# A graph network layer pair on one core: the last stage's linear product moved into the second edge layer

## The chip, the cores and the metric

The kernel runs on 1 core of one Trainium2 chip. The metric is the device time of one execution in microseconds, median of several.

## The reference, cut to what matters

12,500 nodes of 256 numbers, 200,000 edges sorted by destination, 8 heads of 32. A first attention layer over the edges with a feed-forward part gives x. Then:

```
h    = relu(layernorm(x))                      # x: 12500 x 256
h_in = h @ W_lin + b_lin                       # the linear product
feat = (h_in @ W_gat) as 8 heads of 32;  el, er = sums of feat * attn_l, feat * attn_r
e    = leaky_relu(el[src] + er[dst], 0.2)      # 200000 x 8
a    = softmax of e over the edges of one dst
out  = segment_sum(feat[src] * a, dst) + gat_bias
x    = x + h_in + leaky_relu(out, 0.01)
```

All arithmetic is fp32.

## The kernel before

**Stages.** A query, key and value stage over 98 node tiles of 128 nodes (to about 700 us), the first edge layer (to 2750), the node stage with the feed-forward part and the tables of the second layer (to about 3700), the second edge layer (to 5760), the output stage (to 5932).

**Edge layer.** The edges are cut into 782 spans of 256. Work goes in steps, one span against one node tile; a span that straddles two tiles is taken twice, which gives 880 steps in 110 blocks of 8 (`NB`, `ST`). POOL gathers two times 128 rows of `ft_tab` for each span (`gathers`, L531), 1564 gathers a layer, into a ring of 32 spans in `Gf` (`SLOTS`); a slot comes free when the weighed rows of its step are made (`ev_made`). SP loads for each step the row of destinations (`dst_rows`, L452), and passes on to DVE that the rows of a step have landed (`landed`, `rows_rdy`), ten steps behind its loads (`RLAG`). All engines walk the same loop of blocks B and steps s, written out by hand, in order:

- DVE: `el_er` at s (L1218), `members` of step s+6 (L1230), `weigh` of step s-12 (L1287), `add` of step s-14 (L1302), and once a block `leaky` and `scores` at 7, `chunk_scans` of the block before at 0 (L1242), `row_scans` at 1 (L1254), `whole_scans` at 2, `below_maximum` at 3, `rescaled` at 6.
- PE (helpers at L822 and L825): `scores_turned` of the block before at 0, `spread` of step s+2, `agg` of step s-12, then `row_values` at 0, `columns` at 1, `maxima_turned` at 2, `rescale` at 3, `links_turned` at 5.
- ACT (copies at L588): `distances` (L627) and `onehots` (L633) of later steps, `er_rows` of step s+4, `row_values` at 1 (tile `wlf`), `links` at 6 (tile `ats`), and the stores of the sums (L701).

DVE's `chunk_scans` wait for the transposed scores of the block (`s_tr`). PE's `row_values` wait for both scans (`scan_a`), use bank 7, and ACT's `row_values` copy them out for DVE's `row_scans`. Bank 7 also takes `links_turned` (columns 0 to 127), which ACT reads into `ats`.

**Node stage.** It stores for each tile the normalised input transposed (`h2t_tab`) and x with b_lin added (`xm_tab`).

**Output stage.** For each tile ACT loads a tile of `xm_tab` and of `h2t_tab` (L809, L810), six tiles ahead (`FR`); SP loads the sums (L479). PE forms the linear product out of two halves and adds `xm` with the identity as third product, into bank t % 3. DVE divides the sums by their denominator (L1460, L1469, L1478), POOL adds the bias (L582), DVE makes the leaky relu (L1473) and adds PE's bank (L1466) into one of three output buffers; ACT stores it (L816).

Of the kernel before, what the change touches and what calls it, by code (L numbers as in the profile page):

```python
# [22 lines left out]
ALU = mybir.AluOpType  # L23
# [30 lines left out]
RLAG = (6, 10)  # L54
FR = 6
assert all(m * DIV >> 16 == m // SLOTS[0] for m in range(NS))
assert NB % 2 == 0 and NB >= 6 and NS > NSPAN + NT - 1
# [80 lines left out]
def build(nc, x, last, edges, span_src, Wq, Wk, Wv, Wp, bp, g1, b1n, g2, b2n, W1, b1, W2, b2,  # L138
          Wl, bl, Wg, al, ar, gb, out):
    ctx = ExitStack()  # L140
    with ctx:
# [14 lines left out]
        xm_tab = dram("xm_tab", (NPAD, D))  # L156
        h2t_tab = dram("h2t_tab", (NPAD, D))
        sums = dram("sums", (NS * P, HV))
        dst_tab = dram("dst_tab", ((LC * P + 1) * SPAN,))
# [100 lines left out]


        used[0] = 0
        w_l = steps[:, 0:2 * D].rearrange("p (k n) -> p k n", k=2)
        v_gb = steps[:, 2 * D:3 * D]
        fin_h = [carve(D) for _ in range(FR)]
        fin_in, fin_xm = [[carve(w) for _ in range(FR)] for w in (HV, D)]
        fin_a, fin_b, fin_p, fin_o, fin_d = [[carve(w) for _ in range(3)] for w in (D, D, D, D, 2 * H)]
# [15 lines left out]
        for name in """const_made gather_free stats_made setup_loaded path_dve path_pe w_loaded  # L283
            q_x0 q_x1 q_x2 q_x3 q_dve q_rstd q_relu q_tr q_hT q_mm q_ka q_st0 q_st1 q_st2 q_st3 q_vq
            rec_ld rec_f slots sel_made x_mm x_cp fields mask_made er_made tables span_rdy rows_rdy
            m_w m_wge m_acc m_h m_x m_dve0 m_dve1 m_dve2 m_var1 m_var2 m_var3 m_rs1 m_rs2 m_rs3
            m_tr0 m_tr1 m_tr2 m_cp0 m_cp1 m_cp2 m_mm0 m_mm1 m_mm2 m_w1 m_gelu f_tr f_cp f_mm f_w
            m_sxm m_sh2 m_sft m_rdacc m_fo m_xmb f_lin m_xb m_hb m_h1b f_in0 f_in1 f_in2 f_in3 f_in4 f_in5 f_max f_rec f_att f_bias f_lr f_out f_st0 f_st1 f_st2""".split():
            S_[name] = sem(name)
# [44 lines left out]
        def _(sp):  # L334
# [119 lines left out]
            def span_rows(b):  # L454
# [3 lines left out]
                    skip_runtime_bounds_check_because="a step's span is one of the spans or the one after them")[1]  # L458

            sp.wait_ge(S_["rec_ld"], 16 * (LC + 1))  # L460
            for u in range(NS + RLAG[1]):
                if u < NS:
                    if u % ST == 0:
                        at = span_rows(u // ST)
                    dst_rows(Blk(u // ST, 1), u % ST, at[u % ST])
# [5 lines left out]
            for par in range(2):  # L471
                sp.wait_ge(acs[1][par], 32 * (NB // 2))


# [111 lines left out]
        def _(act):  # L586
# [110 lines left out]
            def sum_store(layer, B, h):  # L697
# [4 lines left out]
                              acc[:, B.par, 4 * h:4 * h + 4, :]).then_inc(acs[layer][B.par], 16)  # L702

            def er_rows(B, s):

# [4 lines left out]
            def edge_phase(layer):  # L710
                def turn(B):
                    A = B.on(-1)
                    for s in range(ST):
# [33 lines left out]
                        if s == 3 and A.live:  # L747
                            weights(A)

                z = Blk(0, layer)  # L750
# [53 lines left out]

            for t in range(NT + FR):
                if t < NT:
                    k = t % FR
                    wait(act, S_["f_lin"], t - FR + 1)
                    act.dma_start(fin_xm[k], xm_tab[t * P:(t + 1) * P, :]).then_inc(S_[f"f_in{k}"], 16)  # L809
                    act.dma_start(fin_h[k], h2t_tab[t * P:(t + 1) * P, :]).then_inc(S_[f"f_in{k}"], 16)  # L810
                u = t - FR
                if u < 0:
# [7 lines left out]
        def _(pe):  # L820
# [90 lines left out]
            def scores_turned(B):  # L911
                pe.wait_ge(E_["smade"], B.c + 1)
                tr(bank[6][:, 1:P + 1], S[:, :]).then_inc(E_["s_tr"], 1)

            def row_values(B):

                pe.wait_ge(E_["scan_a"], 2 * B.c + 2)
                for q, v in enumerate((wa[:, 0:1], scan1[:, P - 1:P], scan2[:, 0:1])):
# [21 lines left out]
            def edge_phase(layer):  # L940
                def turn(B):
                    A = B.on(-1)
                    for s in range(ST):
# [20 lines left out]
                        if s == 5 and B.live:  # L964
                            links_turned(B)

                z = Blk(0, layer)
# [73 lines left out]
            edge_phase(1)  # L1041

            for t in range(NT):
                k = t % FR
                o = bank[t % 3][:, 0:D]
                pe.wait_ge(S_[f"f_in{k}"], 48 * (t // FR + 1))
                wait(pe, S_["f_out"], t - 2)
                for c in range(2):
                    mm(o, fin_h[k][:, c * P:(c + 1) * P], w_l[:, c, :], c == 0, False)
                mm(o, ident[:, :], fin_xm[k], False, True).then_inc(S_["f_lin"], 1)  # L1050

        @block.vector
        def _(dve):
# [400 lines left out]
            def f_turn(t):  # L1456
                if t < NT:
                    k, d, src = t % FR, fin_d[t % 3], hv(fin_in[t % FR])
                    dve.wait_ge(S_[f"f_in{k}"], 48 * (t // FR + 1))
                    V.tensor_scalar(d[:, 0:H], src[:, :, HD], 1e-30, None, ALU.max).then_inc(S_["f_max"], 1)  # L1460
                if t >= 3:
                    u = t - 3
                    dve.wait_ge(S_["f_lin"], u + 1)
                    dve.wait_ge(S_["f_lr"], u + 1)
                    wait(dve, S_[f"f_st{u % 3}"], 16 * (u // 3))
                    V.tensor_tensor(fin_o[u % 3], fin_p[u % 3], bank[u % 3][:, 0:D], ALU.add).then_inc(S_["f_out"], 1)  # L1466
                if t < NT:
# [51 lines left out]
```

## Time and profile before

| | |
|---|---|
| median of 3 runs | 7285.09 us (7285.01 to 7289.17) |
| span of the profiled execution, first to last instruction | 5932.0 us |
| time of the profiled execution around its span | not shown; median less span is 1353.1 us |
| PE busy | 5400.5 us, 91% |
| DVE busy | 4947.5 us, 83% |
| POOL busy | 3753.2 us, 63% |
| ACT busy | 3081.2 us, 52% |
| mean granted TensorE clock | 0.896 |
| moved by DMA | 1313.63 MB, 221 GB/s |

How to read it: the profile is of one execution and covers 5932.0 us of it. Engines are PE (TensorE; PEld its weight loads), DVE (VectorE), ACT (ScalarE), POOL (GpSimd) and SP (SyncE, which here issues DMAs only). A name with q, as ACTq, is the engine's queue: it issues a DMA or waits. The ends of matmul records are modelled, so their durations overlap the next ones; their starts are as recorded. An fp32 product shows as two records. Granted clock 1.00 is 2.4 GHz, 0.50 is 1.2 GHz. Idle time has the name of what ended it; "issue" is time in which the engine waited for nothing that the profile shows.

### The profile page before, as it was taken

The numbers are of one execution on the slowest core, as the hardware profiler recorded it, in microseconds if no ns is written. First come the engines' busy times: TensorE is split into PE (matmuls) and PEld (weight loads), VectorE is DVE, ScalarE is ACT, GpSimd is POOL, SyncE is SP. The second block draws the span as 40 slices with busy tenths as digits, with TensorE's granted clock in tenths as the row PEclk, the third lists the DMA queues.
The fourth block names the chain that finished last, engine by engine and source line by source line (L and its number), as shares of the span: only waits on it lengthen the run. The fifth ranks groups of instructions, "written<-read, shape, count | busy, mean of one in ns | idle before, by whom it ended". The sixth has DMA issues, their size and how long they took to land. (4 is left out here: it accounts for less than half of the span.)

```text
span 5932.0 us, 127571 instructions
## 1 busy us (share of the span) xinstructions
PE 5400.5 (91%) x25898; PEld 4282.1 (72%) x25898; DVE 4947.5 (83%) x12562; ACT 3081.2 (52%) x10078; POOL 3753.2 (63%) x4022
## 2 busy tenths in 40 slices
PE   8978888888888888887999998999999999999988
PEld 5556666666666666666999997777777777777766
DVE  4469999999999999996777775788787788887878
ACT  3445666666666666652333334555565565555540
POOL 1147667767766766653444445777777777777754
PEclk9999999999999999998999998777777777777779
DMA  5669898989998988873222223777777787777869
GB/s 176 212 222 293 280 288 286 292 283 287 286 286 285 288 284 283 281 255 100 83 85 85 83 85 109 213 224 221 220 218 218 218 221 219 222 219 220 220 198 311
DMA packets 723029, 1313.63 MB, mean 221 GB/s; under 512 B 109087, under 2 KB 502131, under 8 KB 722420
## 3 DMA queue, kind: packets, MB, share of 16 engines
q0 software_dynamic: 200192, 634.41, 37.8%
q1 hardware_dynamic: 416578, 396.48, 22.3%
q10 hardware_dynamic: 105650, 276.43, 12.3%
q14 instruction: 448, 3.67, 0.2%
q8 instruction: 161, 2.64, 0.2%
HBM read 964.16 MB, written 342.73 MB: 220 GB/s over the span
## 5 line engine op out<-in xcount | busy, mean ns | idle before, releaser
L822 PE MATMUL bank<-ev,oh 128*128 128x264 f32 x7040 | 2303.2, 457 | 88.8 <-DVE ev L1287 88.3
L531 POOL DMA_INDIRECT Gf<-kv_tab,srcs x1564 | 1582.7, 1012 | 710.4 <-issue 496.7
L531 POOL DMA_INDIRECT Gf<-ft_tab,srcs x1564 | 1592.6, 1018 | 484.1 <-issue 411.3
L822 PEld LDWEIGHTS bank<-ev,oh 128*128 128x128 f32 x7040 | 1474.2, 222 | 347.0 <-DVE ev L1287 124.0
L1287 DVE TENSOR_TENSOR ev<-Gf,ex 128x528 f32<-128x528 f32 x1760 | 1228.5, 698 | 1.6 <-ACT ex L695 1.2
L822 PE MATMUL bank<-Gf 128*128 128x128 f32 (+3 forms) x6284 | 1193.7, 343 | 4.5 <-ACT Gf L588 3.3
L822 PE MATMUL bank<-qs,oht 128*128 128x256 f32 x3520 | 955.7, 394 | 226.7 <-DVE prod L1196 226.4
L627 ACT ACTIVATE absd<-lane,dlocs 128x128 f32<-128x128 f32 x3520 | 1112.7, 389 | 3.8 <-DVE bms L1169 3.8
L822 PEld LDWEIGHTS bank<-Gf 128*128 128x128 f32 x6284 | 935.4, 191 | 170.4 <-issue 98.4
L822 PEld LDWEIGHTS bank<-qs,oht 128*128 128x128 f32 x3520 | 599.6, 190 | 437.1 <-issue 371.4
L1302 DVE SCALAR_TENSOR_TENSOR acc<-acc,same,bank 128x264 f32<-128x264 f32 x1540 | 732.3, 475 | 31.5 <-PE bank L822 28.6
L508 POOL TENSOR_TENSOR vr<-vr,mhalf 128x1 f32<-128x1 f32 x392 | 248.6, 634 | 717.1 <-DVE vr L1378 418.6
L633 ACT ACTIVATE oh<-absd,ones 128x512 f32<-128x512 f32 x880 | 631.6, 718 | 10.9
L1196 DVE TENSOR_TENSOR prod<-Gf,bank 128x512 f32<-128x512 f32 x880 | 594.9, 676 | 18.6 <-SPq L395 18.3
L1202 DVE TENSOR_REDUCE sred<-prod 128x16 f32<-128x512 f32 x880 | 590.5, 671 | 0.3
L588 ACT ACTIVATE oht<-bank 128x512 f32<-128x512 f32 x440 | 261.1, 594 | 299.3 <-PE bank L825 296.1
L822 PEld LDWEIGHTS bank<-erq,prod 128*128 128x128 f32 x1760 | 362.5, 277 | 68.4 <-issue 33.2
L777 ACT ACTIVATE Gf<-bank,Gf 128x128 f32<-128x128 f32 x784 | 223.5, 368 | 290.9 <-PE bank L822 290.9
L822 PE MATMUL bank<-erq,prod 128*128 128x8 f32 x1760 | 351.9, 310 | 19.8 <-DVE sred L1218 19.2
L659 ACT ACTIVATE rm<-bank,oh 128x8 f32<-128x8 f32 x220 | 78.6, 357 | 530.2 <-PE bank L822 524.2
L822 PEld LDWEIGHTS bank<-erq,oht 128*128 128x128 f32 x1760 | 270.0, 213 | 58.3 <-issue 25.9
L670 ACT ACTIVATE ats<-bank 128x128 f32<-128x128 f32 x220 | 61.0, 277 | 468.6 <-PE bank L825 468.6
(158 smaller groups left out, 6134.7 us busy)
## 6 DMA issues: line engine op xcount, KB each, us to landing
sums<-acc ACTq DMA_DIRECT2D x440, 528.0 KB
qs<-q_tab SPq DMA_DIRECT2D x880, 128.0 KB
qs<-dst_tab SPq DMA_DIRECT2D x880, 128.0 KB
Gf<-sums SPq DMA_DIRECT2D x196, 132.0 KB, 2.6
kv_tab<-Gf SPq DMA_DIRECT2D x98, 260.0 KB, 2.1
Gf<-in_x SPq DMA_DIRECT2D x196, 128.0 KB, 2.2
Gf<-kv_tab,srcs POOLq DMA_INDIRECT x1564
Gf<-ft_tab,srcs POOLq DMA_INDIRECT x1564
```

The lines of the kernel that those rows point to most:

```text
L508: pool.tensor_tensor(vr[:, 2 * k + 1:2 * k + 2], vr[:, 2 * k:2 * k + 1], mhalf[:, :], ALU.pow).then_inc(done, 1)
L531: pool.indirect_dma_start(out=rows[layer][:, m % SLOTS[layer], k, :], out_offset=None, in_=tab, in_offset=bass.IndirectOffsetOnAxis(ap=src ...
L588: act.activation(o, i_, ACT.Copy).then_inc(s, 1)
L627: act.activation(absd[:, g % 2, k, :], lane[:, :], ACT.Abs, scale=-1.0, bias=dloc[:, B.n, 4 * g + k:4 * g + k + 1]).then_inc(E_["ohd"], 1)
L633: act.activation(oh[:, (B.c * 4 + g) % OHG, :, :].rearrange("p c n -> p (c n)"), absd[:, g % 2, :, :].rearrange("p c n -> p (c n)"), ACT.R ...
L659: act.activation(rm[:, B.par, :], bank[7][:, 392:392 + H], ACT.Identity, scale=oh0[:, B.par, 0:1], bias=oh0[:, B.par, 1:2]).then_inc(E_["r ...
L777: act.activation(gT[:, f * P:(f + 1) * P], bank[2 + f // 4][:, (f % 4) * P:(f % 4 + 1) * P], ACT.Gelu, bias=v_b1[:, f:f + 1]).then_inc(S_[ ...
L822: return nc.tensor.matmul(o, a, r, start=first, stop=end)
L1196: V.tensor_tensor(prod[:, s % 2, :, :], step_rows(0, at)[:, :, 0:D], bank[2 + s % 2][:, :].rearrange("p (k n) -> p k n", k=2), ALU.mult).t ...
L1202: V.tensor_reduce(hc(sred[:, :])[:, :, 2 * s:2 * s + 2].rearrange("p h c -> p c h"), prod[:, s % 2, :, :].rearrange("p k (h w) -> p k h w" ...
L1287: V.tensor_tensor(weighed(B, s).rearrange("p k (h w) -> p k h w", h=H), val.rearrange("p k (h w) -> p k h w", h=H), hc(ex[:, B.par, :])[:, ...
L1302: V.scalar_tensor_tensor(acc[:, B.par, s, :], prev, same[:, B.n * ST + s:B.n * ST + s + 1], sums_bank(B, s), ALU.mult, ALU.add).then_inc(E ...
```

## The change

The three products of a tile are formed in the second edge layer, one tile a block: PE at the end of step 7 into bank 7, ACT copies them to SBUF at the end of its step 7, SP stores them to a new table `r_tab` and loads the inputs two tiles ahead. The output stage loads `r_tab`, eight tiles ahead, in place of `xm_tab` and `h2t_tab`, and DVE adds it from SBUF.

```diff
+RR = ST
+        r_tab = dram("r_tab", (NPAD, D))
+        used[0] = SLOTS[1] * 2 * WIDTH[1]
+        res_h, res_xm, res_o = [[carve(D) for _ in range(2)] for _ in range(3)]
...
-        fin_h = [carve(D) for _ in range(FR)]
-        fin_in, fin_xm = [[carve(w) for _ in range(FR)] for w in (HV, D)]
+        fin_in, fin_r = [[carve(w) for _ in range(n)] for n, w in ((FR, HV), (RR, D))]
...
@@ block.sync
+            def res_turn(b):
+                if b >= 0:
+                    sp.wait_ge(S_["res_cp"], b + 1)
+                    sp.dma_start(r_tab[b * P:(b + 1) * P, :], res_o[b % 2]).then_inc(S_[f"res_st{b % 2}"], 16)
+                t = b + 2
+                if 0 <= t < NT:
+                    for v, tab in ((res_h, h2t_tab), (res_xm, xm_tab)):
+                        sp.dma_start(v[t % 2], tab[t * P:(t + 1) * P, :]).then_inc(S_[f"res_in{t % 2}"], 16)
             for u in range(NS + RLAG[1]):
+                if u % ST == 0 and u // ST - 3 < NT:
+                    res_turn(u // ST - 3)
...
@@ block.scalar
+            def residual(t):
+                act.wait_ge(S_["res_mm"], t + 1)
+                wait(act, S_[f"res_st{t % 2}"], 16 * (t // 2))
+                copy(res_o[t % 2], bank[7][:, 0:D], S_["res_cp"])
...
+                        if s == 7 and layer == 1 and B.n < NT:
+                            residual(B.n)
...
-            for t in range(NT + FR):
+            for par in range(2):
+                act.wait_ge(S_[f"res_st{par}"], 16 * (NT // 2))
+            for t in range(NT + RR):
                 if t < NT:
-                    k = t % FR
-                    wait(act, S_["f_lin"], t - FR + 1)
-                    act.dma_start(fin_xm[k], xm_tab[t * P:(t + 1) * P, :]).then_inc(S_[f"f_in{k}"], 16)
-                    act.dma_start(fin_h[k], h2t_tab[t * P:(t + 1) * P, :]).then_inc(S_[f"f_in{k}"], 16)
+                    k = t % RR
+                    wait(act, S_["f_out"], t - RR + 1)
+                    act.dma_start(fin_r[k], r_tab[t * P:(t + 1) * P, :]).then_inc(qld[k], 16)
...
@@ block.tensor
+            def residual(t):
+                pe.wait_ge(S_[f"res_in{t % 2}"], 32 * (t // 2 + 1))
+                pe.wait_ge(E_["ats_made"], NB + t + 1)
+                o = bank[7][:, 0:D]
+                for c in range(2):
+                    mm(o, res_h[t % 2][:, c * P:(c + 1) * P], w_l[:, c, :], c == 0, False)
+                mm(o, ident[:, :], res_xm[t % 2], False, True).then_inc(S_["res_mm"], 1)
             def row_values(B):
+                if B.layer == 1:
+                    pe.wait_ge(S_["res_cp"], min(B.n + 1, NT))
...
+                        if s == 7 and layer == 1 and B.n < NT:
+                            residual(B.n)
...
@@ block.tensor, the output stage
-            for t in range(NT):
-                k = t % FR
-                o = bank[t % 3][:, 0:D]
-                pe.wait_ge(S_[f"f_in{k}"], 48 * (t // FR + 1))
-                wait(pe, S_["f_out"], t - 2)
-                for c in range(2):
-                    mm(o, fin_h[k][:, c * P:(c + 1) * P], w_l[:, c, :], c == 0, False)
-                mm(o, ident[:, :], fin_xm[k], False, True).then_inc(S_["f_lin"], 1)
@@ block.vector
-                    dve.wait_ge(S_[f"f_in{k}"], 48 * (t // FR + 1))
+                    dve.wait_ge(S_[f"f_in{k}"], 16 * (t // FR + 1))
-                    dve.wait_ge(S_["f_lin"], u + 1)
+                    dve.wait_ge(qld[u % RR], 32 * NB + 16 * (u // RR + 1))
-                    V.tensor_tensor(fin_o[u % 3], fin_p[u % 3], bank[u % 3][:, 0:D], ALU.add)
+                    V.tensor_tensor(fin_o[u % 3], fin_p[u % 3], fin_r[u % RR], ALU.add)
```

## Rows read from the trace of the kernel before

**Rows 1.** The page: its span, and the granted clock in 40 equal slices.
```profile
span 5932.0 us, 127571 instructions
PEclk9999999999999999998999998777777777777779
```

**Rows 2.** Windows: busy us of PE, PEld, DVE, ACT, POOL; clock, DMA share, GB/s.
```profile
3700.00:4900.00 1200.00, 1121.98 (x4681) 889.79 (x4680) 958.18 (x2719) 705.22 (x2595) 924.14 (x906) 0.73 0.78 219
4900.00:5725.00 825.00, 776.75 (x3243) 616.42 (x3242) 665.25 (x1886) 487.32 (x1793) 634.94 (x624) 0.72 0.79 219
...
5800.00:5900.00 100.00, 92.20 (x384) 68.03 (x384) 84.35 (x319) 0.00 (x0) 46.44 (x64) 1.00 1.03 336
```

**Rows 3.** Waits, 4900 to 5725 us: who for whom, us in total, times, longest.
```profile
POOL Gf L531 <- issue: 162.2, 532, 0.3
...
DVE scan L1242 <- PE bank L825: 59.8, 44, 1.9
DVE sred L1218 <- PE bank L822: 45.5, 100, 0.8
...
PE bank L822 <- DVE ev L1287: 33.0, 132, 0.6
...
DVE sred L1218 <- SPq L395: 4.0, 10, 0.7
```

**Rows 4.** Tile S, 3700 to 5760 us: count, ns min/median/max, first and last start.
```profile
L825 PE MATMUL bank<-ident,S x109: 272/273/421, 3703.4 to 5744.0; 128*128 128x128 f32 x109
```

**Rows 5.** Windows over one and a half blocks, cut where the granted clock changes.
```profile
4792.80:4803.00 10.20, 9.85 (x31) 7.72 (x30) 8.70 (x24) 3.98 (x14) 8.07 (x8) 0.50 0.77 198
4803.00:4813.20 10.20, 9.09 (x54) 7.20 (x52) 8.57 (x27) 8.59 (x32) 7.76 (x9) 1.00 0.87 261
4813.30:4823.50 10.20, 10.18 (x30) 8.14 (x31) 7.95 (x23) 4.36 (x18) 7.76 (x9) 0.50 0.69 194
```

**Rows 6.** Timeline of PE around a block's end: start us, us, what, records.
```profile
4804.98 1.14 PE L822 MATMUL bank<-ev,oh 128*128 128x264 f32 x4
4805.95 0.27 PE L825 MATMUL bank<-ident,S 128*128 128x128 f32 x1
...
4807.40 0.27 PE L825 MATMUL bank<-ident,wa 128*1 128x128 f32 x1
```

**Rows 7.** Timeline of DVE and ACT there; in brackets the idle time before.
```profile
4806.26 0.42 DVE L1242 TENSOR_TENSOR_SCAN scan<-ats,bank 128x128 f32<-128x128 f32 x1 [1.18 <-PE bank L825]
4806.36 1.26 ACT L627 ACTIVATE absd<-lane,dlocs 128x128 f32<-128x128 f32 x4
...
4807.93 0.48 ACT L588 ACTIVATE wlf<-bank 1x384 f32<-1x384 f32 x1 [0.20 <-PE bank L825]
```

**Rows 8.** Timeline of PE in the output stage, one tile and the next.
```profile
5911.38 1.09 PE L822 MATMUL bank<-steps,Gf 128*128 128x256 f32 x4
5912.31 0.59 PE L822 MATMUL bank<-Gf,ident 128*128 128x256 f32 x2
5912.74 1.10 PE L822 MATMUL bank<-steps,Gf 128*128 128x256 f32 x4
```

**Rows 9.** Groups of PE, 3700 to 5740 us: busy us, mean ns, idle before.
```profile
L822 PE MATMUL bank<-ev,oh 128*128 128x264 f32 x3455 | 1356.5, 530 | 82.0 <-DVE ev L1287 81.8
```

**Rows 10.** Groups, 0 to 700 us: ACT's copies of 128x256 out of PSUM.
```profile
L588 ACT ACTIVATE Gf<-bank 128x256 f32<-128x256 f32 x196 | 68.4, 373 | 22.9 <-PE bank L822 22.8
```

**Rows 11.** Tile out: issues of its stores, ns min/median/max, first and last start.
```profile
L816 ACTq DMA_DIRECT2D out<-Gf x98: 338/443/1090, 5773.3 to 5925.1; - x98
```

**Rows 12.** Waits of SP's queue, 3760 to 5740 us.
```profile
SPq L395 <- POOLq L538: 881.1, 494, 5.6
```

**Rows 13.** Timeline of DVE in the output stage: the first instruction of two turns.
```profile
5911.95 0.16 DVE L1460 TENSOR_SCALAR Gf<-Gf 128x8 f32<-128x8 f32 x1
...
5913.38 0.16 DVE L1460 TENSOR_SCALAR Gf<-Gf 128x8 f32<-128x8 f32 x1
```

More of the change, by code:

```diff
@@ L287, in build @@
             m_tr0 m_tr1 m_tr2 m_cp0 m_cp1 m_cp2 m_mm0 m_mm1 m_mm2 m_w1 m_gelu f_tr f_cp f_mm f_w
-            m_sxm m_sh2 m_sft m_rdacc m_fo m_xmb f_lin m_xb m_hb m_h1b f_in0 f_in1 f_in2 f_in3 f_in4 f_in5 f_max f_rec f_att f_bias f_lr f_out f_st0 f_st1 f_st2""".split():
+            m_sxm m_sh2 m_sft m_rdacc m_fo m_xmb m_xb m_hb m_h1b f_in0 f_in1 f_in2 f_in3 f_in4 f_in5 res_in0 res_in1 res_mm res_cp res_st0 res_st1 f_max f_rec f_att f_bias f_lr f_out f_st0 f_st1 f_st2""".split():
             S_[name] = sem(name)
@@ L472, in _ @@
                 sp.wait_ge(acs[1][par], 32 * (NB // 2))
+                sp.wait_ge(S_[f"res_st{par}"], 16 * (NT // 2))
             def f_load(t):
@@ L803, in _ @@
             edge_phase(1)
-            for t in range(NT + FR):
+            for par in range(2):
+                act.wait_ge(S_[f"res_st{par}"], 16 * (NT // 2))
+            for t in range(NT + RR):
                 if t < NT:
-                    k = t % FR
-                    wait(act, S_["f_lin"], t - FR + 1)
-                    act.dma_start(fin_xm[k], xm_tab[t * P:(t + 1) * P, :]).then_inc(S_[f"f_in{k}"], 16)
-                    act.dma_start(fin_h[k], h2t_tab[t * P:(t + 1) * P, :]).then_inc(S_[f"f_in{k}"], 16)
-                u = t - FR
+                    k = t % RR
+                    wait(act, S_["f_out"], t - RR + 1)
+                    act.dma_start(fin_r[k], r_tab[t * P:(t + 1) * P, :]).then_inc(qld[k], 16)
+                u = t - RR
                 if u < 0:
@@ L1462, in f_turn @@
                     u = t - 3
-                    dve.wait_ge(S_["f_lin"], u + 1)
+                    dve.wait_ge(qld[u % RR], 32 * NB + 16 * (u // RR + 1))
                     dve.wait_ge(S_["f_lr"], u + 1)
                     wait(dve, S_[f"f_st{u % 3}"], 16 * (u // 3))
-                    V.tensor_tensor(fin_o[u % 3], fin_p[u % 3], bank[u % 3][:, 0:D], ALU.add).then_inc(S_["f_out"], 1)
+                    V.tensor_tensor(fin_o[u % 3], fin_p[u % 3], fin_r[u % RR], ALU.add).then_inc(S_["f_out"], 1)
                 if t < NT:
```

## Prediction, made before the changed kernel ran

> **What bounds the kernel now.** I read the page first, for the span and the slices of the clock, then the busy times by stretch, then in the stretch that gets new work the waits, the order of one block and the clock, and last the stretch that loses work. The span is 5932.0 us [rows 1] and the median of the runs is 7285.09 us. The profile shows nothing of the 1353.1 us between the two; I take them as unchanged, so all sums are made on the 5932.0 us and added to 7285.09. About 0.2%, 15 us, is what a measurement of this kernel can tell from no change.
>
> The second edge layer runs from about 3700 to 5760 us and the output stage from there to the end. In the layer [rows 2] PE is busy 94% of the time (776.75 of 825 us), DVE 81%, POOL 77%, ACT 59%, the DMA engines 79%. Two paces lie very close together. POOL starts 624 gathers in 825 us, one each 1.322 us; its idle time is almost all "issue", 532 times 0.3 us, a fixed pause [rows 3]. So POOL runs without a stop: 1564 gathers in 110 blocks are 14.2 a block, 18.8 us. The consumers have their own pace: the scores of a block are transposed 109 times between 3703.4 and 5744.0 us, one each 18.9 us [rows 4]. Are they held back by the rows that POOL brings? From 4900 us on, no: DVE waits for rows 4.0 us in 825, but for PE 59.8 us in chunk_scans (L1242) and 45.5 us in el_er (L1218) [rows 3]. A later PE would not be hidden by a wait for data.
>
> PE in turn waits 33.0 us in these 825, for DVE's weighed rows [rows 3], and half of its time it is slow: 10.2 us at granted clock 0.50 (1.2 GHz), 10.2 us at 1.00 (2.4 GHz), 10.2 at 0.50 again, once each block [rows 5]. PE is busy 9.85 and 10.18 of 10.20 us at half clock, and starts 31 and 30 records there against 54 at full clock. The order in a block: DVE makes the scores, PE transposes them at the top of step 0, and DVE has stood idle for it 1.18 us when its scan starts at 4806.26 [rows 6, 7]. PE had no idle time there: it was in the aggregation of step 7, at 4804.98, until the transposition at 4805.95. So from about step 4 to step 0 of the next block PE sets the time, and around steps 1 to 3 DVE does.
>
> **The change, part by part.**
>
> *PE, in the layer.* Three products per tile are added at the end of step 7, in 98 of 110 blocks: exactly ahead of the transposition for which DVE waits. Price: at full clock the same six records start 1.36 us before the next tile's (5911.38 to 5912.74) [rows 8]. 98 x 1.36 = 133 us. Ends: at half clock twice that, 2.72 us a block, 267 us (the aggregation's mean of 530 ns over the layer [rows 9], against records 0.24 us apart at full clock in rows 6, shows what half clock does); and nothing, if the products slip into PE's waits. I take full clock, since in the traced block the clock had risen at 4803.0, three microseconds before the place where they go in [rows 5, 6], and I take the whole price, since PE has no wait just ahead of that place and DVE has one just behind it.
>
> *ACT, in the layer.* At the end of step 7 it waits for the products and then copies 128x256 out of PSUM. The copy of that shape took 373 ns [rows 10]: 98 x 0.37 = 37 us on an engine that is busy 59%. Behind this wait on ACT's queue are step 0's four distances (1.26 us) and one er copy, and then row_values, for whose copy DVE waits next. In the traced block row_values found ACT idle for 0.20 us [rows 7]. With the products PE's row transpositions come 1.36 us later, at 4808.8, and ACT, which goes on only at about 4807.4, needs 0.4 + 1.3 + 0.2 us and gets there at 4809.3, where it would have been on time with PE at 4809.3 (4807.93 plus 1.36). It is a tie; I cost it at nothing, with up to 0.3 us a block, 29 us, as its bound, and not below nothing.
>
> *PE's new waits.* The wait for ats_made is for a copy that ACT makes right after step 5's transposition. Behind it would queue all of PE, but ACT waits for that transposition and not the reverse. The wait in row_values for the copy out of bank 7 comes after one spread and one aggregation, 1.45 us by rows 6 (4805.95 to 4807.40), and the copy needs 0.5: covered. If ACT were late, PE would stand there and DVE's scan of the row behind it.
>
> *SP.* A block gets one wait, one store and two loads of 128 KB, some 0.45 us of SP each, as on ACT [rows 11]. Ahead of the change SP waits 881 us of the layer for landings [rows 12], so 1.4 us a block lie in that. The wait for res_cp of block b stands ahead of step 8b+24 on SP. To have passed the dst load of step 8b+23 SP needs the membership rows that DVE makes at step 8b+9, and DVE is there only after the scan of step 8b+8, which waits for a transposition that PE makes behind the products of block b: the copy is out or nearly so, and SP hardly waits. What is queued behind it are dst loads and the notice of landed rows, and DVE would wait for both. 384 KB in 19 us add 21 GB/s to 219 GB/s at a DMA share of 0.79 [rows 2]: 0.07 of share, hidden behind a lookahead of six steps and more.
>
> *POOL.* Nothing is added. With consumers 1.36 us a block slower, POOL's lead grows until the ring of 32 spans is full, and it then waits: that costs nothing, for the consumers set the end.
>
> *Output stage.* Removed per tile: three products, one load of 128 KB of two, a wait of DVE for PE. Stores go out from 5773.3 to 5925.1, 97 intervals of 1.565 us [rows 11]. In that time a tile moves 516 KB (132 of sums, three of 128), at 336 GB/s and a share of 1.03 [rows 2]: the transfers fill the engines. Afterwards it moves 388 KB, which at that rate is 1.18 us a tile. Late next is DVE: its five instructions follow each other without a gap, L1460 at 5911.95 and again at 5913.38, 1.43 us [rows 13]; ACT's queue, three issues of 0.44 us [rows 11], goes to two. So 1.43 for 1.565: 98 x 0.135 = 13 us saved. Ends: nothing, if the stores' landing still holds DVE through the three output buffers, and 24 us, if DVE's 84.35 us busy in 100 us [rows 2] (64 tiles, 1.32 each) could be closed up. The last add now reads SBUF in place of PSUM; I leave its time. The first load of sums waits for the layer's last stores as before.
>
> Sum: 133 - 13 = 120 us, so 7285 + 120 = 7405 us.
>
> **The clock, by a rule.** The trace has the clock rise once a block while PE is busy all the time at 1.2 GHz, and fall after the stretch where DVE sets the pace [rows 5]. So the clock answers to what PE does, and the new products are six dense records. The Trainium skill, "TensorE: Matmul & The Clock Gate", in its part on the clock gate, says that the slow clock is the resting state and that sustained matmul activity releases it. By that rule more work in a block could buy more time at 2.4 GHz. What speaks against much of it here: the products are put in where the clock is mostly up already, and the stretch behind which it falls, steps 1 to 3, keeps its gaps.
>
> **The rivals.**
>
> *A. The clock pays part of it.* Mean clock 0.72 [rows 2] is 56% of the time at half clock, 10.5 us of a block. If that fell to one half of the time, 9.4 us, PE would gain 0.55 us a block and 0.81 would be left: 98 x 0.81 - 13 = 66, 7351 us. For it: the rule above and the clock's answer to load. This is the rule's own outcome; I give it 0.14.
>
> *B. The products are hidden, and the kernel is faster.* Place: PE's waits for DVE between steps 1 and 3, with DVE's waits for rows in the first half of the layer. If PE catches up inside them, or the clock gives all of it back, the layer stays at POOL's 18.8 us a block and only the output stage counts: 7285 - 13 = 7272, at best 7261. It decides from the point where the 1.36 us are made good before the next block's transposition; PE's waits of 33.0 us in 44 blocks are 0.75 a block, too little alone. 0.10.
>
> *C. The products run at half clock.* If the clock's rise comes after step 7 in most blocks, each costs 2.72 us: 267 - 13 = 254, 7539 us. For it: 56% of the time is at half clock; against: [rows 5, 6]. 0.10.
>
> *D. It is not only PE.* ACT's wait or SP's three DMAs delay the chain by another 0.3 us a block: 120 + 29 = 149, 7434 us. 0.16.
>
> **How the numbers follow.** The forecast, full clock and whole price, has 0.50: 7405 us, its own range 7370 to 7440 (1.0 to 1.7 us a block, with both ends of the output stage's gain). Range 7320 to 7480: it holds the forecast, D, nearly all of A, and C where only part of the blocks are slow; left out are B and C proper. Faster by over 0.2% needs B with more than 15 us: 0.07. Within 0.2%: the rest of B and the low end of A: 0.07. Slower: 0.86.
>
> **What would show it.** Scores transposed each 20.2 us in place of 18.9; DVE's wait at L1242 up from 1.4 us a block (59.8 in 44) to about 2.7; the same clock pattern; POOL waiting for DVE's weighed rows from the middle of the layer; output stores 1.43 us apart at some 270 GB/s, and PE silent there. Wrong if transpositions stay 18.9 us apart (B), if the mean clock of the layer is well over 0.72 (A), if the new records take over 400 ns (C), or if ACT's wlf copy or DVE's el_er waits more while PE idles (D).

## The result and the profile after

The changed kernel took 7306.81 us (median of 5, 7302.19 to 7330.29), the kernel before, beside it, 7285.01 us (median of 5, 7270.14 to 7289.17): a ratio of 1.0044, 95% interval 1.0029 to 1.0059. That is 22 us slower by the medians, 21 to 43 by the interval. I had said 7405 us and at least 7320. The sign is right, the size by the medians is a fifth of the 120 us that I gave.

One thing must be known to read the numbers. The kernel before takes one of two times: about 7290 us in this result and in the first set of experiments, which ran on one chip, about 5940 us on the two other chips of the later sets. The trace that I had read (span 5932.0 us [rows 1]) is of the second kind, the times beside it are of the first. I call them the slow and the quick chip; that it is the chip, and not something else that differs between the sets, is not shown. Each ratio is against runs of the kernel before in the same set. Single executions fall out on a quick chip too: of the kernel before one of 16 took 6083.7 us at a mean granted clock of 0.794, of the step 2 kernel below one of 11 took 17555.13 us at 0.28, and the ratios leave both out. The first view is the changed kernel's page, its span and the granted clock in 40 slices:

```profile
span 7328.5 us, 128076 instructions
...
PEclk9978898889888998889999976666776666766675
```

That execution took 7330.29 us, so 1.8 us lie around its span, and not 1353.1. The missing 1353 us are inside the span. The page of the kernel before, run again unchanged on the slow chip (median 7295.63 us, this execution 7308.77), says the same:

```profile
span 7306.9 us, 127571 instructions
...
PEclk9978898889988988898999985666666666666679
```

Its second edge layer (slices 25 to 38) is at 0.5 to 0.6 where [rows 1] has 0.7 (slices 26 to 39). How far apart the blocks are, is in tile S: the line of DVE's mask of the scores, once a block (count, ns min/median/max, first and last start). After, on the slow chip:

```profile
L1241 DVE TENSOR_TENSOR S<-slk,bms x110: 277/284/340, 4402.9 to 7136.1; 128x128 f32<-128x128 f32 x110
```

Before, on the slow chip:

```profile
L1211 DVE TENSOR_TENSOR S<-slk,bms x110: 278/284/339, 4411.2 to 7117.6; 128x128 f32<-128x128 f32 x110
```

109 intervals of 25.1 us against 24.8, where [rows 4] had 18.9: the layer grew by 26.8 us (2733.2 less 2706.4), and blocks are 5.9 us longer on this chip already without the change. Each figure is of one traced execution; the same layer without products took 2698.6 us in the trace of the output stage alone, so the growth is known to some 8 us. Where much of that lies is seen at a block's end, in the timeline of the changed kernel (start us, us, engine, line; in brackets the idle time before and what ended it):

```profile
5514.39 1.14 PE L849 MATMUL bank<-ev,oh 128*128 128x264 f32 x4
...
5515.36 1.03 PE L849 MATMUL bank<-steps,Gf 128*128 128x256 f32 x4
...
5516.23 0.59 PE L849 MATMUL bank<-Gf,ident 128*128 128x256 f32 x2
...
5516.66 0.27 PE L852 MATMUL bank<-ident,S 128*128 128x128 f32 x1
...
5519.22 0.95 POOL L549 DMA_INDIRECT Gf<-ft_tab,srcs  x1 [0.30 <-issue]
5521.70 0.38 ACT L606 ACTIVATE Gf<-bank 128x256 f32<-128x256 f32 x1 [6.78 <-remote]
5521.74 0.42 DVE L1272 TENSOR_TENSOR_SCAN scan<-ats,bank 128x128 f32<-128x128 f32 x1 [7.40 <-remote]
```

The three products (lines 2 and 3) start 1.30 us before the transposition of the scores, near the 1.36 priced from [rows 8]. But then ACT and DVE do nothing for 4.8 us: the transposition is over at 5516.93, and both ACT, which waits for the products, and DVE, which waits for the transposition, start at 5521.7. PE's records go on to 5518.3 and POOL's gathers to 5520.2; after that all four engines stand. The wait's releaser is given as "remote", a name that no wait in the trace of [rows 3] has. It stands where the instruction that gives the signal had ended long before it. The semaphore events in the trace show the signals themselves: those of the products and of the transposition come at 5521.68 and 5521.72, though their records end at 5516.82 and 5516.93. Many blocks have such a pause, in the first edge layer too (its 109 intervals take 2902.2 us here, 431.2 to 3333.4, and 2274.7 on a quick chip). In the waits of 4500 to 7100 us (engine, name and line, releaser: us in total, times, longest) the changed kernel has

```profile
POOL Gf L549 <- DVE ev L1317: 654.3, 213, 7.6
...
DVE scan L1272 <- remote: 338.2, 51, 8.8
...
DVE scan L1272 <- PE bank L852: 112.4, 29, 5.8
```

and the kernel before, there,

```profile
POOL Gf L531 <- DVE ev L1287: 620.7, 203, 7.5
...
DVE scan L1242 <- remote: 387.1, 64, 8.7
...
DVE scan L1242 <- PE bank L825: 41.2, 22, 4.1
```

So before, POOL already waited for the consumers (in [rows 3] nearly all of its idle time was "issue"), and the "remote" pause at the scores was longer and more frequent before than after. Some of it only changed its name: with the rows named PE and the 27.0 and 53.5 us of "issue" at this scan, DVE waits there 455.3 us before and 504.1 after, 0.5 us a block more for products of 1.30. The change filled part of a hole that my trace didn't have.

The output stage didn't get shorter. Its stores, after:

```profile
L843 ACTq DMA_DIRECT2D out<-Gf x98: 338/454/1136, 7166.2 to 7321.3; - x98
```

97 intervals of 1.599 us, 1.571 before on this chip (7147.9 to 7300.3) and 1.565 in [rows 11]. I had said 1.43. A stretch of it (columns as in rows 2):

```profile
7180.00:7240.00 60.00, 0.00 (x0) 0.00 (x0) 59.98 (x186) 0.00 (x0) 33.88 (x38) 0.50 0.85 246
```

The transfers came down from a share of 1.03 to 0.85 and PE is silent, both as forecast; DVE fills the whole time.

### The profile page after: what moved, and what is told of

It reads as the page before. It is cut to its first block and busy times, and to the rows that moved or that the text cites. A ratio compares the mean times of both kernels' runs of the same rounds, so it can differ in the third digit from the quotient of the medians.

```text
span 7328.5 us, 128076 instructions
## 1 busy us (share of the span) xinstructions
PE 5826.4 (80%) x25898; PEld 4585.5 (63%) x25898; DVE 4999.3 (68%) x12562; ACT 3123.1 (43%) x10176; POOL 3704.4 (51%) x4022
## 3 DMA queue, kind: packets, MB, share of 16 engines
q1 hardware_dynamic: 458914, 435.04, 20.2%
## 5 line engine op out<-in xcount | busy, mean ns | idle before, releaser
L849 PE MATMUL bank<-ev,oh 128*128 128x264 f32 x7040 | 2500.1, 489 | 101.1 <-DVE ev L1317 71.3
L549 POOL DMA_INDIRECT Gf<-kv_tab,srcs x1564 | 1502.6, 961 | 1450.6 <-DVE ev L1317 938.6
L849 PEld LDWEIGHTS bank<-ev,oh 128*128 128x128 f32 x7040 | 1593.0, 240 | 400.3 <-DVE ev L1317 103.3
L849 PE MATMUL bank<-qs,oht 128*128 128x256 f32 x3520 | 1037.7, 421 | 225.6 <-issue 136.2
L849 PEld LDWEIGHTS bank<-qs,oht 128*128 128x128 f32 x3520 | 663.7, 210 | 426.9 <-issue 346.6
L852 PE MATMUL bank<-ident,oh 128*128 128x128 f32 x1760 | 317.6, 309 | 247.4 <-ACT oh L651 218.1
L1272 DVE TENSOR_TENSOR_SCAN scan<-ats,bank 128x128 f32<-128x128 f32 x220 | 91.6, 417 | 609.8 <-remote 429.7
L849 PEld LDWEIGHTS bank<-erq,prod 128*128 128x128 f32 x1760 | 391.6, 299 | 72.8 <-issue 46.9
L849 PEld LDWEIGHTS bank<-erq,oht 128*128 128x128 f32 x1760 | 319.9, 249 | 178.5 <-issue 141.0
L606 ACT ACTIVATE Gf<-bank 128x256 f32<-128x256 f32 (+1 forms) x494 | 185.0, 385 | 570.8 <-remote 290.0
```

What stands on the lines that cost most here:

```text
L549: pool.indirect_dma_start(out=rows[layer][:, m % SLOTS[layer], k, :], out_offset=None, in_=tab, in_offset=bass.IndirectOffsetOnAxis(ap=src ...
L606: act.activation(o, i_, ACT.Copy).then_inc(s, 1)
L849: return nc.tensor.matmul(o, a, r, start=first, stop=end)
L852: return nc.tensor.transpose(o, i_, ident[:, :])
L1272: V.tensor_tensor_scan(scan1[:, :], ats[:, 0:P], bank[6][:, 1:P + 1], -BIG, ALU.add, ALU.max).then_inc(E_["scan_a"], 1)
```

## The experiments

### On the slow chip: the kernel before, the output stage alone, the products twice

**The kernel before, unchanged**, for its profile beside the changed one's.

> The kernel before, unchanged, for a trace taken like that of the changed kernel, whose span of 7328.5 us covers its whole time while the first trace of before covered 5932.0 of 7285. Theory P (the products lie whole on the path of PE in the layer): the layer takes some 90 to 130 us less here than in the changed kernel, and the output stage that much more than in it. Theory H (most of their price is covered by something that the first trace of before did not show): pauses in which all engines stand still, every 26 us as in the changed kernel, are here too, the blocks take within 0.5 us of the changed kernel's, and the output stage has stores 1.57 us apart.

Measured 7295.63 us, ratio 1.0002 (0.9988 to 1.0016). Its rows stand above: the time is inside the span, the pauses are there without the change, and the blocks are within 0.25 us of the changed kernel's, as theory H had it.

**The output stage alone.** Nothing is added to the layer, and the stage loads `xm_tab` where the changed kernel loads `r_tab`; the product with `W_lin` is left out of the result.

```diff
-                if u % ST == 0 and u // ST - 3 < NT:
-                    res_turn(u // ST - 3)
...
-                        if s == 7 and layer == 1 and B.n < NT:
-                            residual(B.n)
...
-                    act.dma_start(fin_r[k], r_tab[t * P:(t + 1) * P, :]).then_inc(qld[k], 16)
+                    act.dma_start(fin_r[k], xm_tab[t * P:(t + 1) * P, :]).then_inc(qld[k], 16)
```

> Nothing added in the layer; the output stage as changed, with the table of x loaded in place of the products, so the output lacks the product with W_lin. Theory P in its prediction: before less 13 us, 7272, stores 1.43 us apart. Rival, from the changed kernel's trace (POOL's add 909 ns there against 725, DVE's leaky relu 814 against 458, now that DVE's last add reads SBUF twice): no gain, before plus 0 to 4 us, stores 1.60 us apart.

Measured 7281.67 us, ratio 0.9986 (0.9971 to 1.0001). Stores 7119.9 to 7275.6, 1.605 us apart, where this chip had 1.571 before. The time alone can't decide, since 13 us less (0.9982) lies in its interval; the stores do: three products, a 128 KB load and a wait taken out of each tile bring nothing.

**The products twice**, all else as in the changed kernel.

```diff
+                for lap in range(2):
                     for c in range(2):
                         mm(o, res_h[t % 2][:, c * P:(c + 1) * P], w_l[:, c, :], c == 0, False)
-                mm(o, ident[:, :], res_xm[t % 2], False, True).then_inc(S_["res_mm"], 1)
+                    m = mm(o, ident[:, :], res_xm[t % 2], False, True)
+                m.then_inc(S_["res_mm"], 1)
```

> The changed kernel with the three products of each block formed twice in the layer (the second time over the first, same result). Theory P: another 1.36 us a block, the changed kernel plus 133 us, 7440. Theory H, if what covers them has room: plus 0 to 50 us; if the room is used up by the first three: 100 to 133 us.

Measured 7351.01 us, ratio 1.0088 (1.0066 to 1.0111). Tile S:

```profile
L1243 DVE TENSOR_TENSOR S<-slk,bms x110: 279/284/347, 4396.0 to 7146.1; 128x128 f32<-128x128 f32 x110
```

The layer takes 2750.1 us: 26.8 us more than before with the products once, 43.7 with them twice, 0.27 and 0.45 us for each tile in place of 1.36 and 2.72. Two things eat the rest. First the pause: from the start of the transposition to the start of DVE's scan, the mean over the blocks between 4500 and 7100 us, taken from the two lines' starts, is 3.48 us before, 2.68 after, 1.96 with the products twice, and 0.31 to 0.32 in the kernel before and the changed one on the quick chips. The waits of this kernel for the scores:

```profile
DVE scan L1274 <- remote: 288.7, 39, 8.9
...
DVE scan L1274 <- PE bank L852: 195.3, 46, 7.0
```

With 61.5 us of "issue" that is 545.5 us, after 455.3 before and 504.1 with the products once: DVE's wait grows by 0.5 and 0.9 us a block, for 1.30 and 2.60 us of products. Second the clock. The window 4500 to 7100 us (columns as in rows 2) of the kernel before:

```profile
4500.00:7100.00 2600.00, 2120.61 (x7762) 1650.44 (x7762) 1600.33 (x4509) 1172.85 (x4301) 1504.43 (x1467) 0.65 0.60 166
```

The same window of the changed kernel:

```profile
4500.00:7100.00 2600.00, 2183.07 (x8221) 1718.33 (x8220) 1574.86 (x4451) 1188.64 (x4333) 1502.63 (x1460) 0.68 0.64 178
```

And with the products twice:

```profile
4500.00:7100.00 2600.00, 2215.97 (x8679) 1751.22 (x8678) 1546.67 (x4392) 1171.85 (x4276) 1497.27 (x1452) 0.71 0.63 177
```

0.65, 0.68, 0.71: some 460 records more each time, and a higher clock each time (the layer of the output stage alone, without products, has 0.64 there). Of the 1.30 us of a tile 0.80 come off the pause, 0.27 remain, and 0.23 are left for the clock; twice it is 2.60, 1.52, 0.45 and 0.63. The first three of each are read or counted, the last is what is left over: that it is the clock is argued from these three rows, not shown by itself.

### On a quick chip: which part of the layer costs

The next two sets ran on two chips where the kernel before takes 5938.19 us (median of 11) and 5938.80 (of 27). **The changed kernel itself** there:

> The changed kernel itself, once more. There are two conditions of the same program: the kernel before took 7285 to 7292 us where the changed kernel was first timed, and 5938 us where the runs with the layer part alone (+2.4%) and PE alone (+2.4%) were made. If this chip gives before near 5938, the layer part (+144) and a stage that gives nothing back make the changed kernel 5938 + 140 to 150 = 6080 to 6090, a block of 20.3 us. If it gives before near 7290, the changed kernel is 20 to 45 us slower, as first timed.

Measured 6084.88 us, ratio 1.0245 (1.0231 to 1.0259): 146 us slower. Tile S:

```profile
L1241 DVE TENSOR_TENSOR S<-slk,bms x110: 278/285/350, 3683.4 to 5884.7; 128x128 f32<-128x128 f32 x110
```

20.2 us apart for 18.9, to the digit what I had named; the layer takes 2201.3 us, 143 more than the 2057.9 of the kernel before (3684.8 to 5742.7 in its first trace). The waits, 4900 to 5725 us:

```profile
DVE scan L1272 <- PE bank L852: 116.7, 41, 3.1
...
POOL Gf L549 <- DVE ev L1317: 85.5, 86, 2.6
```

2.85 us a block at the scan (1.36 in [rows 3], "about 2.7" forecast), and POOL waits for DVE's weighed rows.

**The layer's part alone**: all of it as changed, with the output stage of before. **The products alone**: the kernel before, with three products out of the identity and `w_l` in that place, which nobody reads; no load, no copy, no store.

```diff
+            def residual(t):
+                pe.wait_ge(E_["ats_made"], NB + t + 1)
+                o = bank[7][:, 0:D]
+                for c in range(2):
+                    mm(o, ident[:, :], w_l[:, c, :], c == 0, False)
+                mm(o, ident[:, :], w_l[:, 0, :], False, True)
...
+                        if s == 7 and layer == 1 and B.n < NT:
+                            residual(B.n)
```

> Products, copy, store and loads in the layer as changed; the output stage as before, with its own products. Theory P: before plus 133 us, 7425. Theory H (the products fall into a time in which DVE waits for the transposed scores anyway, and a higher granted clock pays more of them): before plus 20 to 45 us; the output stage is worth less than 5 us either way, so this is within 10 us of the changed kernel.

> The kernel before with three products of the same size added on PE at the end of step 7 of 98 blocks, from tiles that lie in SBUF and into bank 7, read by nobody: no copy, no store, no loads, and no wait for the copy ahead of the row transpositions. If PE alone makes the cost of the changed layer, this is before plus 20 to 45 us, as the run with the whole layer part. If the copy on ACT or the DMAs on SP make it (case D of the prediction), it is before plus 0 to 10 us.

Measured: layer alone 6082.79 us, 1.0243 (1.0230 to 1.0256); products alone 6078.79 us, 1.0239 (1.0226 to 1.0253), and once more in the last set 6080.40 us, 1.0234 (1.0220 to 1.0247). By tile S the layer with the products alone takes 2201.8 us (3686.6 to 5888.4), as in the changed kernel. Both expectations of 20 to 45 us were made from the slow chip's result, and are missed on this one. Six matmul records a block are the whole cost here; ACT's wait and copy, SP's three DMAs and PE's waits add nothing that shows. Rival D falls on the quick chips; on the slow one it wasn't tested.

**The output stage alone**, as above, on a quick chip:

> Nothing added in the layer; the output stage as changed, with the table of x loaded in place of the products, so the output lacks the product with W_lin. Before plus 0 to 5 us in either condition; stores 1.60 us apart.

Measured 5944.18 us, ratio 1.0009 (1.0000 to 1.0019); stores 5781.5 to 5936.9, 1.602 us apart. Nothing gained here either.

### Why the output stage gains nothing

Groups of the stage, changed kernel on the slow chip (busy us, mean ns, idle before):

```profile
L600 POOL TENSOR_TENSOR Gf<-Gf,steps 128x256 f32<-128x256 f32 x96 | 87.3, 909 | 67.5 <-DVE Gf L1508 67.5
L1503 DVE SCALAR_TENSOR_TENSOR Gf<-Gf 128x256 f32<-128x256 f32 x98 | 79.8, 814 | 0.0
L1496 DVE TENSOR_TENSOR Gf<-Gf 128x256 f32<-128x256 f32 x98 | 41.2, 420 | 0.5 <-DMA out<-Gf 0.3
```

The kernel before, there:

```profile
L582 POOL TENSOR_TENSOR Gf<-Gf,steps 128x256 f32<-128x256 f32 x98 | 71.1, 726 | 161.4 <-DVE Gf L1478 161.4
L1473 DVE SCALAR_TENSOR_TENSOR Gf<-Gf 128x256 f32<-128x256 f32 x98 | 44.2, 451 | 0.0
L1466 DVE TENSOR_TENSOR Gf<-Gf,bank 128x256 f32<-128x256 f32 x98 | 41.1, 419 | 19.3 <-DMA out<-Gf 15.4 <-issue 0.4
```

The last add itself is no slower (420 ns for 419). POOL's bias add beside it goes from 726 to 909 ns and the leaky relu behind it from 451 to 814. **The PSUM variant** tests it: the changed kernel, but ACT copies each loaded tile of `r_tab` into a PSUM bank, and DVE adds from there, as it did before.

```diff
+                c = t - RR + 2
+                if 0 <= c < NT:
+                    act.wait_ge(qld[c % RR], 32 * NB + 16 * (c // RR + 1))
+                    wait(act, S_["f_out"], c - 2)
+                    copy(bank[c % 3][:, 0:D], fin_r[c % RR], S_["res_cp"])
...
-                    dve.wait_ge(qld[u % RR], 32 * NB + 16 * (u // RR + 1))
+                    dve.wait_ge(S_["res_cp"], NT + u + 1)
...
-                    V.tensor_tensor(fin_o[u % 3], fin_p[u % 3], fin_r[u % RR], ALU.add)
+                    V.tensor_tensor(fin_o[u % 3], fin_p[u % 3], bank[u % 3][:, 0:D], ALU.add)
```

> The changed kernel with ACT copying each loaded tile of products into a PSUM bank, from which DVE adds it, as it did before the change. If DVE and POOL hold each other up when both read two operands from SBUF (POOL's add 909 ns in the changed kernel, 725 before), POOL's add is back at 725 to 750 ns, DVE's leaky relu at some 460, the stores are 1.43 to 1.5 us apart, and the kernel is 10 to 16 us faster than the changed one. If the stage is held by something else, stores stay 1.60 us apart and the time is the same.

Measured 6076.31 us, 1.0231 (1.0218 to 1.0245). Its groups:

```profile
L600 POOL TENSOR_TENSOR Gf<-Gf,steps 128x256 f32<-128x256 f32 x95 | 68.6, 723 | 148.8 <-DVE Gf L1513 148.8
L1508 DVE SCALAR_TENSOR_TENSOR Gf<-Gf 128x256 f32<-128x256 f32 x93 | 45.0, 484 | 0.0
...
L1501 DVE TENSOR_TENSOR Gf<-Gf,bank 128x256 f32<-128x256 f32 x92 | 38.5, 418 | 17.5 <-DMA out<-Gf 13.2 <-ACT bank L606 3.2 <-issue 0.3
```

POOL is back at 723 ns, the relu at 484, and the stores come 1.496 us apart (5921.6 to 6066.7), 11 us less in the stage than the changed kernel's 1.609 (5914.1 to 6070.2) there. It is still not 1.43: DVE waits 13.2 us again for stores to land, the end of the saving that I had named. The kernel's time is 8.6 us under the changed kernel's, which was measured in the next set, and the intervals of the two ratios overlap; so the 10 to 16 us expected are not confirmed, and the gain is read from the stores. The two timelines show how the engines meet. Changed kernel, quick chip:

```profile
5991.30 0.41 DVE L1496 TENSOR_TENSOR Gf<-Gf 128x256 f32<-128x256 f32 x1
5991.38 0.91 POOL L600 TENSOR_TENSOR Gf<-Gf,steps 128x256 f32<-128x256 f32 x1 [0.69 <-DVE Gf L1508]
...
5991.75 0.83 DVE L1503 SCALAR_TENSOR_TENSOR Gf<-Gf 128x256 f32<-128x256 f32 x1
```

PSUM variant, two turns of the relu, the first with no POOL instruction beside it:

```profile
5991.52 0.37 DVE L1508 SCALAR_TENSOR_TENSOR Gf<-Gf 128x256 f32<-128x256 f32 x1
...
5992.22 0.41 DVE L1501 TENSOR_TENSOR Gf<-Gf,bank 128x256 f32<-128x256 f32 x1
5992.30 0.72 POOL L600 TENSOR_TENSOR Gf<-Gf,steps 128x256 f32<-128x256 f32 x1 [1.22 <-DVE Gf L1513]
...
5992.66 0.64 DVE L1508 SCALAR_TENSOR_TENSOR Gf<-Gf 128x256 f32<-128x256 f32 x1
```

The relu takes 0.37 us alone; with POOL's add in flight it ends just after that add's end: 5993.30 for 5993.02, and 5992.58 for 5992.29 in the changed kernel. In the changed kernel DVE's add, now with two operands in SBUF, starts 0.08 us ahead of POOL's, which takes 0.19 us longer than in the variant; the relu behind it then lies under POOL's add for longer. The Trainium skill, "SBUF — State Buffer", section "Who interferes with whom", has the rule: a DVE instruction with two SBUF inputs contends with a GpSimd instruction that reads SBUF, and the one that comes second waits. The trace agrees in who is slowed and by what, with 726 and 909 ns for POOL, 451 and 814 for DVE, and the PSUM variant takes both back.

### Another place for the products

**Step 0.** The changed kernel with the products behind the transposition of the scores, at step 0 of the next block, ahead of `row_values`.

```diff
-                        if s == 7 and layer == 1 and B.n < NT:
-                            residual(B.n)
...
+                            if layer == 1 and A.n < NT:
+                                residual(A.n)
                             row_values(A)
```

> The changed kernel with the products moved behind the transposition of the scores: PE forms them in step 0 of the next block, after its aggregation and ahead of the row transpositions, and ACT copies at the end of its step 0. PE stands there for DVE's second scan (258 us in 2600 in the trace of the kernel before). Theory P: the place is no better, since PE is the bound; the changed kernel within 10 us. Theory H: the products lie in PE's wait and the scores are no longer held up by them: the changed kernel less 15 to 40 us.

Measured 6243.16 us, 1.0505 (1.0483 to 1.0527): 158 us worse than the changed kernel (timed in the next set; by the ratios 2.6% of the kernel before), where theory H had a gain on it and theory P a difference of 10 us. Both are wrong. The waits, 4900 to 5725 us:

```profile
DVE scan L1272 <- PE bank L852: 86.0, 37, 3.2
DVE U L1284 <- ACT wlf L606: 74.5, 37, 2.0
...
PEld bank L852 <- ACT Gf L606: 32.4, 37, 0.9
```

The wait at the scan is still there, 2.3 us a block, and a second one of 2.0 us stands behind it, for `row_values`, which in the whole layer of the changed kernel is 0.4 us. Up to 0.9 us of it is no product: `row_values` writes bank 7 too, and stands here straight behind the products, so PE waits for ACT's copy out of that bank. The stretch's clock is 0.69 (0.75 in the changed kernel) and the blocks are 21.8 us apart (3688.9 to 6066.1). It moved the products from one step of DVE's chain to the next, put ACT's copy into that chain, and lost clock besides; what each costs is not separated.

**Step 2.** There PE waits for DVE's maxima before it can go on, and behind this sparse stretch the clock falls [rows 5]. The products go to the end of PE's step 2 of the next block, into bank 0; ACT copies them at the end of its step 3.

```diff
-                pe.wait_ge(E_["ats_made"], NB + t + 1)
-                o = bank[7][:, 0:D]
+                wait(pe, S_["res_cp"], t)
+                o = bank[0][:, 0:D]
...
                         if s == 2 and A.live:
                             maxima_turned(A)
+                            if layer == 1 and A.n < NT:
+                                residual(A.n)
...
-                        if s == 7 and layer == 1 and B.n < NT:
-                            residual(B.n)
```

> The changed kernel with the products at the end of PE's step 2 of the next block, behind the transposed maxima, into bank 0 which nothing else uses in this layer, and the copy at the end of ACT's step 3. There PE waits for DVE, and behind that stretch the granted clock falls in each block. Theory clock: dense records there keep the clock up for longer; near 5938 the block goes from 20.3 us back to 18.8 or a little below, POOL's pace, so 130 to 150 us less than the changed kernel; near 7290 also faster than the changed kernel, by 30 us or more. Rival: PE's queue is late there too, what follows is put back by the whole 1.36 us a block, and the place makes less than 30 us of difference.

> As e10_step2, with ACT's copy of the loaded products into PSUM in the output stage: 7 to 11 us less than e10_step2 (stores 1.50 us apart in e7_psum, 1.60 in the changed stage). By theory clock that is faster than the kernel before by 5 to 20 us.

Measured: step 2 5948.43 us, 1.0013 (1.0004 to 1.0022); with the PSUM variant's output stage as well 5941.78 us, 1.0001 (0.9992 to 1.0010). The same six records a block, 136 us cheaper than in the changed kernel of the same set, as theory clock had it. Against the kernel before the second misses its expectation: it is level, not 5 to 20 us faster. Tile S with the products at step 2:

```profile
L1239 DVE TENSOR_TENSOR S<-slk,bms x110: 275/284/314, 3683.5 to 5755.3; 128x128 f32<-128x128 f32 x110
```

Its waits, 4900 to 5725 us:

```profile
DVE sred L1246 <- SPq L400: 104.6, 97, 3.5
```

Blocks are 19.0 us apart, and DVE now waits 104.6 us for gathered rows (4.0 in [rows 3]): the consumers have become quicker than POOL's 18.8 us. The layer takes 2071.8 us, 13.9 more than before. PE is busy 744.06 of the 825 us, 17.1 us a block, though it has six records more than before, when it was 17.8. Its aggregation shows why. Before, 4900 to 5725 us (busy us, mean ns, idle before):

```profile
L822 PE MATMUL bank<-ev,oh 128*128 128x264 f32 x1403 | 551.7, 531 | 33.0 <-DVE ev L1287 33.0
```

With the products at step 2:

```profile
L849 PE MATMUL bank<-ev,oh 128*128 128x264 f32 x1391 | 478.0, 474 | 27.8 <-DVE ev L1315 27.0
```

The same instructions are 57 ns shorter, which a wait that hides the products would not make them; a higher clock does. Windows cut where it changes, the changed kernel on a quick chip:

```profile
4791.80:4802.00 10.20, 9.80 (x31) 7.76 (x31) 7.89 (x23) 4.21 (x18) 7.76 (x9) 0.52 0.81 226
4802.00:4812.20 10.20, 9.34 (x53) 7.45 (x51) 7.23 (x22) 7.26 (x26) 7.27 (x8) 0.98 0.84 238
```

The same view with the products at step 2:

```profile
4791.40:4798.20 6.80, 6.80 (x25) 5.24 (x24) 5.19 (x16) 4.24 (x15) 5.21 (x6) 0.52 0.77 222
4798.20:4818.70 20.50, 18.28 (x101) 14.86 (x100) 16.96 (x50) 14.20 (x52) 15.93 (x16) 0.99 0.82 239
4818.70:4822.10 3.40, 3.40 (x11) 2.85 (x12) 2.39 (x9) 0.58 (x2) 2.72 (x3) 0.55 0.92 256
```

The changed kernel keeps the pattern of [rows 5], 10.2 us at each level. With the products at step 2 the clock stays at 2.4 GHz for 20.5 us in this block and is down for 3.4 us behind it and 6.8 ahead of it. The means of 4900 to 5725 us are 0.72 before, 0.75 changed, 0.82 here, 0.69 with the products at step 0. The step from 0.72 to 0.75 is no effect of the products: the output stage alone, with none in the layer, has 0.75 there too. The Trainium skill, "TensorE: Matmul & The Clock Gate", section "What's actually happening", says that the slow clock is the default and that activity releases it. The 0.82 agrees; the 0.69 of step 0, with the same records, does not follow from it, so that the place in the block decides is read from these rows alone. How much of the 136 us is the clock and how much PE's waits at that place, no run separates; nor does one keep the products at step 7 and change only their bank, but the products alone, without copy or wait, cost the whole there.

**Once more.** The products alone and the step 2 kernel with the PSUM stage; the expectations name both chips.

> The kernel of e11_step2_psum once more, for the condition in which the kernel before takes near 7290. Near 5938: the same as before within 0.3%, as e11. Near 7290: theory pause (products cost where they hold up the scores' transposition, and nothing where PE waits) gives before less 5 to plus 10 us; theory clock alone, with a granted clock of 0.65 in the layer to raise, gives before less 30 us or more.

> The kernel of e5_pe_only once more, for the same reason. Near 5938: plus 2.4%, as e5. Near 7290: plus 20 to 40 us if PE alone makes the cost of the layer part there too; plus 0 to 10 us if it is the copy and the DMAs.

It ran on a quick one (before 5940.49 us, median of 16): step 2 with PSUM 5939.88 us, 0.9995 (0.9981 to 1.0009), the products alone as given above. So both results stand twice for the quick chips and not at all for the slow one. No version beats the kernel before; the last is level with it.

## Why the prediction was wrong, step by step

**The base.** The step that failed is "The profile shows nothing of the 1353.1 us between the two; I take them as unchanged". They don't lie around the span (1.8 us do) but inside it: of the 5.9 us by which a block of the second layer is longer 3.2 are the pause between the scores' transposition and DVE's scan (3.48 for 0.32 us), and there the change puts its work. What the other 2.7 are isn't shown; the layer's mean clock is 0.65 there for 0.72. A gap of 19% between span and median was a reason to doubt that trace and times are of the same condition, and I gave it no case of its own.

**PE in the layer, 133 us.** Right for the condition of its trace: the layer grew by 143 us on a quick chip, 1.46 us a tile for 1.36, and the products alone give the same. In the timed condition this term was 26.8 us, 0.27 a tile: "I take the whole price, since PE has no wait just ahead of that place and DVE has one just behind it" held only on the quick chip. On the slow one 0.80 of the 1.30 us came out of the pause, and a higher clock is the likely taker of the rest, which no run shows by itself. So rival B's mechanism (hidden) did most and rival A's (the clock pays) some, each in part: their 7272 and 7351 us enclose the 7306.81 measured. The pause that hid the work was in neither. The forecast's own range has a slip too: 7370 to 7440 is 1.0 to 1.7 us a block with the output stage's 13 us at both ends, and not with both ends of its gain, which would give some 7359 to 7452.

**ACT, PE's waits, SP, POOL: nothing.** Right on the quick chips; products alone and the whole layer part differ by 4 us, within the intervals.

**The output stage, -13 us.** Wrong: +3 us (155.1 for 152.4 us of stores). The step is "the last add now reads SBUF in place of PSUM; I leave its time". Its own time did stay; that of the two instructions that share SBUF with it did not, 183 ns on POOL and 363 on DVE. With that undone the stage gains about 7 us on a quick chip (145.1 for 151.8 [rows 11]) and not 13, as the stores' landing holds DVE.

**What would show it.** 20.2 us apart, 2.7 us at L1242 (2.85), the same clock pattern and POOL waiting: all on the quick chip. Stores 1.43 us apart at 270 GB/s: neither (1.599, 246).

Open remain: what makes the pauses on the slow chip (the trace names only "remote"), whether the products alone make the 27 us there, and whether step 2 helps there.

## What to carry to other kernels

Hold the profile's span against the timed median first: traces and times of one execution differed by 1.8 us here, and 1353 us meant that the trace was of another condition, with other waits. Work that moves to TensorE costs by its place: on the quick chips it cost its full length, 143 us of the layer, ahead of a transposition for which VectorE waits, and 14 in the sparse stretch behind which the clock falls. An operand moved from PSUM to SBUF is to be priced at the instructions of GpSimd beside it, not at the add.

## What the hardware showed that I had not expected

- One program takes 5940 us on two chips and 7290 on a third, with the same instructions. In the traced block two engines stand for some 5 us for signals of a third whose records are over. PE's transposition to DVE's scan in the kernel before: 0.32 us on a quick chip, 3.48 on the slow one.
- With six dense records a block more the mean granted clock was 0.82 at one place and 0.69 at another, where it is 0.72 to 0.75 without them.
- A DVE add of unchanged 420 ns, one operand moved to SBUF, made POOL's add 25% and DVE's relu 80% longer.
